# An attention block on one core: where the third load into a staging slot is issued, and how many fill products run

## The chip, the cores and the metric

The kernel runs on one core of a Trainium2 chip. The metric is the device time of one execution in microseconds (us). TensorE (PE) multiplies matrices and loads its weights beside them (PEld); VectorE (DVE), ScalarE (ACT) and GpSimd (POOL) work elementwise; SyncE (SP) issues nearly all transfers. Each engine executes its own list strictly in order and waits at semaphores for the others.

## The reference

The input x is 8 sequences of 512 rows of 256 numbers. Three steps follow each other:

```python
x = x + 0.5 * ffn(layernorm(x))      # layernorm again inside; weights quantised to -1, 0, 1
x = x + attention(layernorm(x))      # 16 query heads, 4 key/value heads, head size 128,
                                     # rotary positions, causal window of 64
x = x + 0.5 * ffn(layernorm(x))      # same ffn weights as in the first step
# ffn(x) = layernorm(x, gamma, beta) @ ternary(weight).T + bias
# attention: softmax(q k.T / sqrt(128), masked) v, then @ Wo + bo
```

## The kernel before, in words

The sequences ("batches") are worked off one after the other, and the work of neighbouring batches is interleaved. A batch is held transposed, features on the 128 partitions. Float32 operands of the large products are split into a rounded high part and a low remainder, and a product takes three matmuls (`three`, L567). The high part of a weight is made by ScalarE (`split_high`, L921), the low one by VectorE or GpSimd (L759, L1024).

The order of the work is written out by hand: one table of steps for each engine (TENSOR, VECTOR, SCALAR, GPSIMD, SYNC, L58 to L207), each with a prologue, a first batch, middle batches, a last batch and an epilogue. A step such as `Q2n` is "query head 2 of the next batch"; `c` is the current batch, `p` the previous, `i` and `f` occur once. `program` (L215) expands a table and the engine walks the list. Nothing is reordered at run time: a step that waits holds up all steps behind it on its engine.

The steps that matter here:

- `K0`, `Q0` to `Q15`: a projection on TensorE into one of two job banks in turn (`rope_job`, L645). VectorE multiplies it by the sine table (`rope_sin`, L802) and then the cosine table (`rope_cos`, L807). SyncE swaps the two halves of `rope_sin` with two DMAs of 128 KB into `rope_swap` (L548), and GpSimd adds both (`rope_add`, L1068). There are four sets of these buffers, used in turn: the fifth projection (Q3 in the prologue) may write its sine product once the first swap has landed, and its cosine product once the first add is done. A TensorE job waits until the job two places before it has been read out of its bank.
- `V00`, `V01`: values, read by ScalarE (L992) and VectorE (L812). `shift0` (L526) waits for V01's low part, then issues four DMAs of 192 KB that copy the values, moved by half a tile, into `v_odd`.
- `S` are scores, `exp` their exponentials on ScalarE, `inv` the reciprocal sums on VectorE, `probs` the normalisation on GpSimd, `T` the transposes of the probabilities on TensorE, `W` the product with the values, `O` the projection with Wo.
- Weights arrive in ten loads of 512 KB (`LOADS`, L414). Loads 0, 8 and 9 share one place, `stage_r` (the buffer `x_res`): load 0 holds the values' weights, load 8 a quarter of Wo, load 9 another. Load 8 may be issued when both splits of load 0 are done (`stage`, L494); the last of these is GpSimd's piece 1 (`w1i`). When load 8 has landed, ScalarE splits it in step `w11f`. The list of ScalarE goes on from the prologue into the first batch as `... w7i V01n | w11f exp0c mask2c exp1c V10c probsT0c`; that of VectorE as `... Q3n V01n | K1c Q4c max0c Q5c max1c inv0c Q6c inv1c w11f`; that of TensorE as `... Q2n Q3n V01n | K1c Q4c Q5c S0c S1c Q6c V10c T0c S2c Q7c W0c`.
- `fill0` to `fill5` (L727): products of ones or of the identity into `heads_p` which nobody reads. Their counts stand in FILLS; each is a float32 matmul that shows as two records. `last_fill` (L736) is a second such helper in the epilogue, between the two transposes `YT0p` and `YT1p`.

Of the kernel before, what the change touches and what calls it, by code (L numbers as in the profile page):

```python
# [37 lines left out]
P = 128  # L38
BATCHES, SEQ, E = 8, 512, 256
# [48 lines left out]
        T14c  # L88
    """,
    "epilogue": """  # L90
        O13p W14p T15p O14p W15p O15p YT0p last_fill0p YT1p FO0p FO1p
    """,
}
VECTOR = {
# [92 lines left out]
}  # L187
SYNC = {
    "prologue": """
        stage8i K0n Q0n Q1n Q2n Q3n shift0n  # L190
    """,
    "first": """
        K1c Q4c Q5c Q6c stage9f Q7c load0n K2c Q8c Q9c Q10c Q11c shift1c K3c
# [13 lines left out]
}  # L207


FILLS = (10, 3, 2, 2, 4, 4)  # L210
PARTS = {"p": -1, "c": 0, "n": 1}
WAVES = ("YT", "FO", "stats", "scale", "norm", "bias")

# [46 lines left out]
def block_kernel(nc, x, wq, wk, wv, wo, ffn_wT, columns, rows, rope_tables, mask, ident, out):  # L260
# [3 lines left out]
    with ExitStack() as ctx:  # L264
        def sb(name, shape, dt=F32):
            return ctx.enter_context(nc.sbuf_tensor(name, shape, dt))

        def psum(name, shape, dt=F32):
            return ctx.enter_context(nc.psum_tensor(name, shape, dt))
# [9 lines left out]
        w_tern = sb("w_tern", [P, EC, E], F32R)  # L279
# [33 lines left out]
        identf = sb("identf", [P, P])  # L313
# [15 lines left out]
        heads_p = psum("heads_p", [P, GROUP, 2, CHUNK])  # L329
# [158 lines left out]
        def flat_heads(ap):  # L488
            return ap.rearrange("p h c q -> p (h c q)")
# [16 lines left out]
        def _(sp):  # L506
# [13 lines left out]
            def store_half(x):  # L520

                _, m, b = x
                sp.wait_ge(ffn_added, FFN_OUT["FO2", m, b] + 1)
                sp.dma_start(out_t[b][:, 2 * m:2 * m + 2, :], x_res[:, 2 * m:2 * m + 2, :]).then_inc(out_stored, 16)

            def shift_values(x):  # L526

                _, half, b = x


                sp.wait_ge(v_lo, VALUES["V", (half, 1), b] + 1)
                cols = slice(half * NKV * HD // 2, (half + 1) * NKV * HD // 2)
                for s in range(2):
                    sp.dma_start(v_odd[0:CHUNK, s, :, cols].bitcast(F32),
                                 v_s[CHUNK:P, s, 0:BLOCKS - 1, cols].bitcast(F32)).then_inc(v_shifted, 16)
                    sp.dma_start(v_odd[CHUNK:P, s, :, cols].bitcast(F32),
                                 v_s[0:CHUNK, s, 1:BLOCKS, cols].bitcast(F32)).then_inc(v_shifted, 16)
# [28 lines left out]
        def _(pe):  # L566
# [160 lines left out]
            def fill(x):  # L727
# [3 lines left out]
                if x[1] >= 2:  # L731
                    pe.wait_ge(ident_in, 16)
                for _ in range(FILLS[x[1]]):
                    nc.tensor.matmul(flat_heads(heads_p[:, :])[:, 0:P], square, square, start=True, stop=True)

            def last_fill(_):  # L736

                dst = flat_heads(heads_p[:, :])
                for _ in range(6):
                    nc.tensor.transpose(dst[0:96, 0:P], identf[:, 0:96], identf[:, :])  # L740
                for _ in range(6):
                    nc.tensor.transpose(dst[0:64, 0:P], identf[:, 0:64], identf[:, :])
                for _ in range(3):
                    nc.tensor.matmul(dst[:, 0:96], identf[:, :], identf[:, 0:96], start=True, stop=True)
                for _ in range(5):
                    nc.tensor.matmul(dst[0:64, 0:E], w_tern[:, 0, 0:64], w_tern[:, 0, :], start=True, stop=True)
                for _ in range(5):
                    nc.tensor.matmul(dst[:, 0:P], w_tern[:, 0, 0:P], w_tern[:, 0, 0:P], start=True, stop=True)

            for x in PE_STEPS:  # L750
                {"S": scores, "T": transpose_probs, "W": values, "O": project, "K": rope_job, "Q": rope_job,
                 "V": value_job, "YT1": transpose_y, "YT2": transpose_y, "XT": transpose_y,
                 "FO1": ffn_job, "FO2": ffn_job, "total": sum_scale, "beta": beta_product,
                 "open": open_banks, "fill": fill, "last_fill": last_fill}[x[0]](x)


        @block.vector
        def _(dve):
            def split_low(x):  # L759
                n = x[1]  # L760
                _, where, dst = PIECES[n]
                dve.wait_ge(split_hi, HIGH[x] + 1)
                nc.vector.tensor_tensor(dst[1], where, dst[0].bitcast(F32), ALU.subtract).then_inc(split_lo_dve, 1)
# [395 lines left out]
```

## Time and profile before

| | us |
|---|---|
| median of 3 runs | 812.55 |
| lowest, highest | 811.66, 813.08 |
| profiled execution | 811.97 |
| its span, first to last instruction | 809.8 |
| TensorE busy | 790.4 (98%) |
| TensorE weight loads | 738.9 (91%) |
| VectorE, ScalarE, GpSimd busy | 634.3, 514.9, 452.8 |
| mean granted TensorE clock | 0.997 |

The profile is one execution; its times are counted from the first instruction. The page's chain of waits is followed back from the last instruction, and gives TensorE 90% of the span. TensorE is not evenly busy: the first and the last of the page's 40 slices, some 20 us each, are the least filled. Busy time of matmuls is modelled at its end, so that a group's duration holds a tail of some 0.2 us that overlaps the next group.

### The profile page before, as it was taken

How to read it: one execution, taken by the hardware profiler on the slowest of the kernel's cores; microseconds unless marked ns; L12 is line 12 of the kernel's file. 1: busy time of each engine (PE TensorE's matmuls, PEld its weight loads, DVE VectorE, ACT ScalarE, POOL GpSimd, SP SyncE). 2: the span in 40 equal slices, each digit the busy share in tenths (PEclk: the TensorE clock that was granted, in tenths of full speed). 3: DMA queues.
4: the chain of work that ended last, by engine and by line, in shares of the span. 5: the costliest groups of instructions: out<-in, count | busy, mean ns of one | idle time of the engine just before them, and what ended most of it. 6: DMA issues, size and time to landing. Idle time of an engine off the chain costs nothing.

```text
span 809.8 us, 16159 instructions
## 1 busy us (share of the span) xinstructions
PE 790.4 (98%) x5720; PEld 738.9 (91%) x5720; DVE 634.3 (78%) x1292; ACT 514.9 (64%) x1633; POOL 452.8 (56%) x437
## 2 busy tenths in 40 slices
PE   7799999999999999999999999999999999999986
PEld 6589999999999999999999999999999999999985
DVE  5588868978788887988778797797878887787754
ACT  4477765676666665676656766567665667575672
POOL 4578635576465645666446664557546464564542
PEclk9999999999999999999999999999999999999999
DMA  8463224341252423333233332344125242424300
GB/s 298 112 163 92 55 47 97 95 115 40 60 137 66 105 53 95 89 80 92 53 91 93 88 83 53 91 100 111 40 64 134 66 105 53 101 57 105 79 1 27
DMA packets 52431, 70.53 MB, mean 87 GB/s; under 512 B 7040, under 2 KB 30080, under 8 KB 52352
## 3 DMA queue, kind: packets, MB, share of 16 engines
q1 hardware_dynamic: 51792, 69.17, 35.2%
q8 instruction: 45, 0.74, 0.4%
q10 hardware_dynamic: 560, 0.34, 0.1%
q14 instruction: 34, 0.28, 0.1%
HBM read 10.76 MB, written 4.19 MB: 18 GB/s over the span
## 4 chain that ended last, share of the span: by engine, by line
PE 90%; POOL 3%; DVE 2%; ACT 2%; issue 2%; DMA 1%; SPq 0%; ACTq 0%; POOLq 0%; DVEq 0%
PE job_p L572 31%; PE attn_p L572 23%; PE scores_p L588 13%; PE heads_p L572 11%; PE probsT_p L626 7%; PE job_p L698 3%; PE job_p L687 3%; ACT headsT L960 1%; DVE headsT L780 1%; DMA k_s<-ffn_wT 1%; ACT y L982 1%; POOL q_s L1068 1%; POOL wq_s L1031 0%; POOL probs L1048 0%; ACT probs L938 0%
## 5 line engine op out<-in xcount | busy, mean ns | idle before, releaser
L1048 POOL TENSOR_TENSOR probs<-probs,inv_sum 128x512 f32<-128x512 f32 x128 | 134.4, 1050 | 198.3 <-DVE inv_sum L774 198.3
L938 ACT ACTIVATE probs<-scores_p,neg_max 128x128 f32<-128x128 f32 x512 | 181.0, 372 | 56.7 <-DVE neg_max L768 56.2
L572 PE MATMUL attn_p<-wo_s,headsT 128*128 128x256 f32 x1536 | 208.8, 285 | 5.0 <-DVE headsT L780 5.0
L572 PE MATMUL job_p<-xnT,wq_s 128*128 128x512 f32 x768 | 205.3, 403 | 0.6 <-DVE v_s L812 0.5
L572 PEld LDWEIGHTS attn_p<-wo_s,headsT 128*128 128x128 f32 x1536 | 195.7, 191 | 11.1 <-DVE headsT L780 6.6
L1068 POOL TENSOR_TENSOR q_s<-rope_cos,rope_swap 128x512 f32<-128x512 f32 x128 | 164.3, 1292 | 48.2 <-DMA rope_swap<-rope_sin 48.2
L960 ACT ACTIVATE headsT<-heads_p,columns_s 128x512 fp32r<-128x512 f32 x128 | 88.2, 689 | 154.5 <-PE heads_p L572 153.0
L572 PEld LDWEIGHTS job_p<-xnT,wq_s 128*128 128x128 f32 x768 | 136.6, 190 | 25.4 <-DVE v_s L812 0.9
L780 DVE SCALAR_TENSOR_TENSOR headsT<-heads_p,columns_s,headsT 128x512 fp32r<-128x512 f32 x128 | 95.7, 748 | 59.7 <-ACT headsT L960 58.2
L588 PE MATMUL scores_p<-k_s,q_s 128*128 128x128 f32 x1024 | 135.0, 275 | 0.0
L802 DVE SCALAR_TENSOR_TENSOR rope_sin<-job_p,columns_s,rope_t 128x512 f32<-128x512 f32 x160 | 119.0, 744 | 14.0 <-PE job_p L572 10.1
L588 PEld LDWEIGHTS scores_p<-k_s,q_s 128*128 128x128 f32 x1024 | 125.9, 192 | 1.6
L807 DVE SCALAR_TENSOR_TENSOR rope_cos<-job_p,columns_s,rope_t 128x512 f32<-128x512 f32 x160 | 118.7, 742 | 0.5 <-POOL k_s L1068 0.5
L938 ACT ACTIVATION_READ_ACCUMULATOR probs<-scores_p,neg_max 128x1 f32 x512 | 108.1, 211 | 0.0
L768 DVE TENSOR_REDUCE neg_max<-scores_p 128x4 f32<-128x512 f32 x128 | 86.8, 682 | 15.8 <-PE scores_p L588 15.8
L786 DVE TENSOR_TENSOR probsT<-probsT_p,probsT 128x512 fp32r<-128x512 f32 x128 | 86.6, 677 | 4.4 <-ACT probsT L966 4.4
L966 ACT ACTIVATE probsT<-probsT_p 128x512 fp32r<-128x512 f32 x128 | 76.4, 597 | 20.8 <-PE probsT_p L626 20.7
L572 PE MATMUL heads_p<-probsT,v_s 128*128 128x256 f32 x480 | 79.0, 284 | 0.0
L953 ACT ACTIVATE scores_p<-mask_s 128x512 f32<-128x512 bf16 x128 | 77.5, 607 | 0.7
L626 PE MATMUL probsT_p<-identf,probs 128*128 128x128 f32 x512 | 77.0, 273 | 0.4 <-POOL probs L1048 0.2
L1068 POOL TENSOR_TENSOR k_s<-rope_cos,rope_swap 128x512 f32<-128x512 f32 x32 | 41.3, 1292 | 49.3 <-DMA rope_swap<-rope_sin 49.3
L572 PEld LDWEIGHTS heads_p<-probsT,v_s 128*128 128x128 f32 x480 | 66.7, 191 | 0.5 <-DVE probsT L786 0.4
(87 smaller groups left out, 930.7 us busy)
## 6 DMA issues: line engine op xcount, KB each, us to landing
rope_swap<-rope_sin SPq DMA_DIRECT2D x320, 128.0 KB, 2.3
v_odd<-v_s SPq DMA_DIRECT2D x64, 192.0 KB, 3.2
out<-x_res SPq DMA_DIRECT2D x16, 256.0 KB, 2.5
x_in<-x SPq DMA_DIRECT2D x15, 256.0 KB, 3.2
staging<-wo SPq DMA_DIRECT2D x2, 512.0 KB, 10.7
staging<-wq SPq DMA_DIRECT2D x2, 512.0 KB, 10.8
x_res<-wo SPq DMA_DIRECT2D x2, 512.0 KB, 4.1
x_res<-wv SPq DMA_DIRECT2D x1, 512.0 KB, 7.3
```

Of the source, the lines that this page charges most:

```text
L572: mm = nc.tensor.matmul(dst, a(p), b(q), start=first and clears and i == 0, stop=last and i == 2, skip_group_check=True)
L588: mm = nc.tensor.matmul(dst[:, 2 * cc + pair, :], q_s[g % 2][:, c, 2 * pair:2 * pair + 2, :], k_s[:, g % 2, w0:w0 + P], start=False, stop= ...
L626: mm = nc.tensor.transpose(probsT_p[:, k, :], probs[:, x[1] % 2, k, :], identf[:, :])
L768: nc.vector.tensor_reduce(neg_max[:, i, :], scores_p[i][:, :, :], AX.X, ALU.max, negate=True).then_inc(max_ready, 1)
L780: nc.vector.scalar_tensor_tensor(out=flat_heads(headsT[:, 1]), in0=flat_heads(heads_p[:, :]), scalar=bv_s[:, g:g + 1], in1=flat_heads(head ...
L786: nc.vector.tensor_tensor(probsT[:, 1, :, :], probsT_p[:, :, :].rearrange("p (c a) n -> p c (a n)", c=2), probsT[:, 0, :, :].bitcast(F32), ...
L802: nc.vector.scalar_tensor_tensor(out=rope_sin[:, r, :], in0=bank[:, :], scalar=bias, in1=sin_t, op0=ALU.add, op1=ALU.mult).then_inc(rope_s ...
L807: nc.vector.scalar_tensor_tensor(out=rope_cos[:, r, :], in0=bank[:, :], scalar=bias, in1=cos_t, op0=ALU.add, op1=ALU.mult).then_inc(rope_c ...
L938: ins = nc.scalar.activation(probs[:, i, k, :], scores_p[i][:, k, :], ACT.Exp, bias=neg_max[:, i, k:k + 1], accum_out=row_sum[:, i, k:k + 1])
L960: nc.scalar.activation(flat_heads(headsT[:, 0]), flat_heads(heads_p[:, :]), ACT.Identity, bias=bv_s[:, g:g + 1]).then_inc(heads_hi, 1)
L1048: nc.gpsimd.tensor_tensor(probs[:, i, :, :], probs[:, i, :, :], inv_sum[:, i, :].unsqueeze(2).to_broadcast([P, 4, P]), ALU.mult).then_inc( ...
L1068: nc.gpsimd.tensor_tensor(roped(x), as_roped(x, rope_cos[:, r, :]), as_roped(x, rope_swap[:, r, :]), ALU.add).then_inc(rope_added, 1)
```

## The change

It has three parts. In SyncE's prologue, the issue of load 8 (`stage8i`) moves from ahead of the five swaps K0n, Q0n to Q3n and of `shift0n` to behind them. In FILLS, fill1 goes from 3 products to 1 and fill2 from 2 to 1. In the epilogue `last_fill` with its 25 products and transposes of several shapes gives way to a plain `fill6` of 12 products of the identity.

```diff
@@ TENSOR, epilogue
-        O13p W14p T15p O14p W15p O15p YT0p last_fill0p YT1p FO0p FO1p
+        O13p W14p T15p O14p W15p O15p YT0p fill6p YT1p FO0p FO1p
@@ SYNC, prologue
-        stage8i K0n Q0n Q1n Q2n Q3n shift0n
+        K0n Q0n Q1n Q2n Q3n shift0n stage8i
@@
-FILLS = (10, 3, 2, 2, 4, 4)
+FILLS = (10, 1, 1, 2, 4, 4, 12)
@@ TensorE's helpers
-            def last_fill(_):
-
-                dst = flat_heads(heads_p[:, :])
-                for _ in range(6):
-                    nc.tensor.transpose(dst[0:96, 0:P], identf[:, 0:96], identf[:, :])
-                for _ in range(6):
-                    nc.tensor.transpose(dst[0:64, 0:P], identf[:, 0:64], identf[:, :])
-                for _ in range(3):
-                    nc.tensor.matmul(dst[:, 0:96], identf[:, :], identf[:, 0:96], start=True, stop=True)
-                for _ in range(5):
-                    nc.tensor.matmul(dst[0:64, 0:E], w_tern[:, 0, 0:64], w_tern[:, 0, :], start=True, stop=True)
-                for _ in range(5):
-                    nc.tensor.matmul(dst[:, 0:P], w_tern[:, 0, 0:P], w_tern[:, 0, 0:P], start=True, stop=True)
-
```

## Rows read from the trace of the kernel before

**Rows 1.** The page: chain of waits, by engine.
```profile
PE 90%; POOL 3%; DVE 2%; ACT 2%; issue 2%; DMA 1%; SPq 0%; ACTq 0%; POOLq 0%; DVEq 0%
```
**Rows 2.** Timeline of SyncE's queue: start, us, line, transfer, count.
```profile
29.26 0.37 SPq L500 DMA_DIRECT2D x_res<-wo  x1
29.67 7.60 SPq L548 DMA_DIRECT2D rope_swap<-rope_sin  x10
37.51 0.65 SPq L534 DMA_DIRECT2D v_odd<-v_s  x1
```
**Rows 3.** Timelines of GpSimd and VectorE (in brackets: idle before, releaser).
```profile
27.86 1.31 POOL L1031 TENSOR_TENSOR wv_s<-x_res,wv_s 128x512 fp32r<-128x512 f32 x1
34.83 1.27 POOL L1068 TENSOR_TENSOR k_s<-rope_cos,rope_swap 128x512 f32<-128x512 f32 x1 [5.66 <-DMA rope_swap<-rope_sin]
40.98 2.42 POOL L1031 TENSOR_TENSOR wq_s<-staging,wq_s 128x1024 fp32r<-128x1024 f32 x1
...
25.69 0.74 DVE L802 SCALAR_TENSOR_TENSOR rope_sin<-job_p,columns_s,rope_t 128x512 f32<-128x512 f32 x1
31.34 0.74 DVE L807 SCALAR_TENSOR_TENSOR rope_cos<-job_p,columns_s,rope_t 128x512 f32<-128x512 f32 x1
34.85 0.75 DVE L802 SCALAR_TENSOR_TENSOR rope_sin<-job_p,columns_s,rope_t 128x512 f32<-128x512 f32 x1 [2.77 <-DMA rope_swap<-rope_sin]
```
**Rows 4.** Timeline of TensorE, same columns.
```profile
32.14 1.69 PE L572 MATMUL job_p<-wv_s,xnT 128*128 128x256 f32 x12
36.94 2.66 PE L572 MATMUL job_p<-xnT,wk_s 128*128 128x512 f32 x6 [3.11 <-DVE rope_cos L807]
42.74 1.95 PE L588 MATMUL scores_p<-k_s,q_s 128*128 128x128 f32 x16
47.70 0.66 PE L626 MATMUL probsT_p<-identf,probs 128*128 128x128 f32 x4
49.00 1.64 PE L572 MATMUL job_p<-xnT,wq_s 128*128 128x512 f32 x6
```
**Rows 5.** Stretches: us, busy of PE, PEld, DVE, ACT, POOL; clock, DMA share, GB/s.
```profile
38.00:40.00 2.00, 2.00 (x6) 1.51 (x6) 0.36 (x1) 0.00 (x0) 2.00 (x3) 0.50 0.83 186
60.00:100.00 40.00, 40.00 (x303) 37.89 (x302) 34.69 (x77) 28.26 (x91) 31.53 (x29) 1.00 0.33 74
```
**Rows 6.** Transfers: issue to landing in us, of 29 to 29.6, 37.4 to 40.2, 49.9 to 50.5.
```profile
x_res<-wo SPq DMA_DIRECT2D x1, 512.0 KB, 4.4
v_odd<-v_s SPq DMA_DIRECT2D x4, 192.0 KB, 3.2
x_res<-wo SPq DMA_DIRECT2D x1, 512.0 KB, 3.8
```
**Rows 7.** The swap buffers in 20 to 60 us.
```profile
DMA to landing us min/median/max: 2.2/2.6/4.5
```
**Rows 8.** Timeline of ScalarE.
```profile
33.87 0.60 ACT L992 ACTIVATE v_s<-job_p 128x512 fp32r<-128x512 f32 x1 [5.36 <-PE job_p L572]
34.36 1.05 ACT L925 ACTIVATE wo_s<-x_res 128x1024 fp32r<-128x1024 f32 x1
44.56 0.37 ACT L938 ACTIVATE probs<-scores_p,neg_max 128x128 f32<-128x128 f32 x1 [9.14 <-DVE neg_max L768]
```
**Rows 9.** Timeline of TensorE and ScalarE at the start.
```profile
6.94 1.63 PE L734 MATMUL heads_p<-y 128*128 128x128 f32 x6
8.36 1.06 PE L687 MATMUL job_p<-identf,y 128*128 128x128 f32 x4
11.33 0.66 PE L687 MATMUL job_p<-identf,y 128*128 128x128 f32 x4 [1.14 <-ACT y L982]
6.75 1.09 ACT L982 ACTIVATE y<-x_in,shift,rstd 128x256 f32<-128x256 f32 x2 [0.37 <-POOL shift L1042]
```
**Rows 10.** Timeline of TensorE at the end.
```profile
796.75 1.70 PE L572 MATMUL attn_p<-wo_s,headsT 128*128 128x256 f32 x12 [1.56 <-DVE headsT L780]
802.83 0.63 PE L687 MATMUL job_p<-identf,y 128*128 128x128 f32 x4 [0.90 <-ACT y L982]
```

More of the change, by code:

```diff
@@ L753, in _ @@
                  "FO1": ffn_job, "FO2": ffn_job, "total": sum_scale, "beta": beta_product,
-                 "open": open_banks, "fill": fill, "last_fill": last_fill}[x[0]](x)
+                 "open": open_banks, "fill": fill}[x[0]](x)
         @block.vector
```

## The prediction

> **What bounds the kernel now.** I read the page's chain of waits first, then stretches of the trace, then each engine's timeline from 20 to 60 us. The chain gives TensorE 90% [rows 1], and from 47.7 us on it is busy without a gap (40.00 of 40.00 us in the stretch to 100) [rows 5]. So a microsecond is only won or lost where TensorE stands still: in the first 48 us, and in the epilogue. What sets the whole time is when the first transpose of probabilities, T0c, starts: 47.70 us [rows 4]; everything behind it keeps its order and its distance.
>
> Before T0c there is one long stall. Load 8 goes out at 29.26, after GpSimd's last split of load 0 (27.86 + 1.31), and the first swap only at 29.67, behind it [rows 2, 3]. That swap had been possible since K0n's sine product, 25.69 + 0.74 = 26.43. It lands so late that GpSimd waits 5.66 us, to 34.83, and VectorE 2.77 us, to 34.85, for the fifth projection's sine product [rows 3]; so TensorE idles 3.11 us ahead of K1c, from 33.83 to 36.94 [rows 4]. After this gap the granted clock falls to 0.50, the 1.2 GHz level (the stretch from 38 to 40), and K1c takes 2.66 us instead of the 1.64 that six such matmuls take at 1.00 [rows 4, 5].
>
> **The change part by part.** *The swaps.* They go out as soon as their sine products exist. A pair costs SP two issues of some 0.6 us (one takes 0.65 in the shift) [rows 2], and a swap lands 2.2 to 2.6 us after its issue, the least and the median [rows 7]. K0n's lands at 26.5 + 0.6 + 2.3 = 29.4 instead of 34.8. GpSimd is busy with its split until 29.2, so the adds begin at 29.4, 5.4 us earlier. VectorE ends Q2n's cosine product at 31.34 + 0.74 = 32.08 [rows 3] and can do Q3n's two at once (0.67 us apart), to 33.53. TensorE ends V01n at 33.83 and goes on with K1c at 33.7: 3.2 us won. The clock has no reason to fall there. K1c and Q4c take 1.4 us each at the full clock (Q4c waits until 35.2 for V01n's low part); Q5c needs K1c's cosine product (36.7) and ends at 38.2. Q3n's swap lands at 35.8 and its add ends at 37.1, in time. S0c starts at 38.2 instead of 42.74, 4.5 us earlier [rows 4]. S1c, Q6c and V10c follow to 43.0: 0.9, half of a group of two less its tail, 1.4, and 1.5 as V01n without its tail [rows 4].
>
> *What load 8 is now late for.* It is issued behind the shift. V01n's high part ends at 33.87 + 0.60 [rows 8], its low part, priced as VectorE's like products at 0.75 [rows 3], at 35.2. The shift's four issues take 4 x 0.65 = 2.6 us [rows 2], so load 8 goes out at 37.8 instead of 29.26. Alone it took 4.4 us to land, its successor 3.8 [rows 6]; here 768 KB of values are ahead of it, the last of them landing at 37.2 + 3.2 = 40.4. Low bound for its landing 37.8 + 3.8 = 41.6; high bound, all of it behind the shift's end and half a swap's lateness more, 43.4. I take 37.8 + 4.5 = 42.3, nearest to the row of the same load.
>
> Nobody needs this piece of Wo soon, but ScalarE's list has its split, w11f, ahead of exp0c. Today w11f runs at 34.36, covered by the wait for the scores, and ScalarE then idles 9.14 us [rows 8]. Now ScalarE stands at w11f from 34.5 to 42.3, although the row maxima of S0c are ready by 40.0. exp0c starts 0.95 us after w11f, at 43.25. Behind exp0c wait inv0c, probs0c and T0c: from 44.56 to 47.70 they took 3.14 us [rows 4, 8]. VectorE and GpSimd offer no shorter way; GpSimd's splits w8i and w7f, 2.4 us each [rows 3], end at 41.9. T0c: 43.25 + 3.14 = 46.4, 1.3 us earlier than now. Of the 4.5 us won at S0c, 3.2 go back at the new wait. With the bounds of the landing: 45.7 to 47.5, a gain of 2.0 to 0.2.
>
> *TensorE meanwhile.* It has nothing from 43.0 to 46.4: the stall of 3.11 us has become one of about 3.4 us, further on. A gap of 3.11 was followed by the low clock; gaps of 1.56 and 0.90 us at the end, with packed work behind the first at its usual 1.70 us, were not [rows 4, 5, 10]. A gap longer than the one that cost the clock most likely costs it again. K1c lost 1.0 us of 2.66 to it and the work behind K1c lost more; half the speed over some 3.4 us, which the low level lasted, is 1.7 us, of which some 0.2 fall on waits that are there anyway: +1.5. Bounds: 0, if the clock stays, and 2.9, if the low level ends later because it begins inside the gap. In the profiled execution the fall cost less, since GpSimd's splits, which end at 45.7 now, would have held T0c until 46.85 anyway.
>
> By the Trainium skill (TensorE: Matmul & The Clock Gate, Part 1), the chip's looks at TensorE's activity are free-running, not tied to the kernel's start; the trace, one execution, neither shows nor denies it. By that rule the fall comes in some executions and not in others, for both kernels, and the sum would lie between the forecast and the first rival.
>
> *The first fills.* Records of fill1 take 0.23 to 0.27 us there. Six hold TensorE from 6.94 to 8.36, while y for YT0n is ready at 6.75 + 1.09 = 7.84 [rows 9]. Two end at 7.5, so YT0n starts at 8.0 and ScalarE and all after it get 0.2 to 0.4 us; none if records are already fast by then. fill2's two missing records lie in the gap ahead of YT1n (1.14 us) and cost nothing themselves. Taken: -0.2.
>
> *The last fill.* Now 29 records, from 798.7 to 801.9; fill6 has 24 of 0.11 us and ends at 801.4. The next transposes wait for y until 802.83 [rows 10]. The old fill was hidden and so is the new: 0. The gap grows from 0.9 to 1.4, below the 1.56 that cost no clock; if it does, FO1p is 1.1 us longer.
>
> Sum on the profiled 811.97 (span 809.8 and 2.17 around it): -1.3 + 1.5 - 0.2 = 0. The profiled execution lies 0.6 under the median, and as the difference is what I predict, I put it on the median: 812.6.
>
> **The rivals.** *1. The clock stays up after the new gap.* For it: at 1.56 us it stayed [rows 10], and the limit may be a matter of luck for a single gap. Against: 3.4 is longer than 3.11. Then -1.3 - 0.2 = -1.5: 811.1, and with the early landing 810.4.
>
> *2. The start stays at the low clock (slower).* The granted column reads 1.00 from the first microsecond, but four transposes take 1.06 us at 8.36 and 0.66 at 11.33 [rows 9]: the level is 1.2 GHz up to then, and rises ahead of 11.33. Before the rise TensorE works without a gap from 6.94 to past 9.4; fill0's ten products, ahead of that, brought none, since fill1's records still take twice their later time [rows 9]. The change takes six records out of this block and opens gaps at 7.5 to 8.0 and from 9.5 to 11.0. If the rise then comes only after the packed stretch from 11 to 17, YT1n takes 0.4 more and the product for beta 0.9 more, both on the path to x_mid, and open0i and fill4i then delay XT0n by some 0.2: +1.5, bound 3. It decides if the first ten products alone don't bring the rise. With the forecast's other terms: 814.3; with a clock that stays up at T0c, 812.8. By the Trainium skill (same page, Part 4: PE-mode transpose) a transpose does not count as busy TensorE like a matmul. By that rule the thinned block, half of it transposes, would hold still less, which speaks for this rival; no row isolates it.
>
> *3. Load 8 lands late.* The swaps of K1c and Q4c and the shift share the engines with it; at 43.4 T0c is at 47.5: +1.1, 813.7. By the Trainium skill (DMA: Bandwidth & Descriptors, Queues, rings and completion order) each engine consumes a queue's descriptors in ring order; the trace agrees, as K0n's swap behind load 8 took 4.5 instead of 2.3 us [rows 7].
>
> *4. The wait at w11f doesn't hold exp0c*, because the landing is much earlier than I think. exp0c would start at 40.1 and T0c at 43.3: -4.4, without a gap, 808.0. Against: the issue cannot come before V01n's low part, 35.2, and four issues.
>
> **How the numbers follow.** Forecast 0.40, rival 1 0.25, rival 2 0.19, rival 3 0.08, rival 4 0.08. A measurement can tell about 0.2%, 1.6 us. Faster by more than that is rival 4 and well over half of rival 1, with the early landings: 0.24. Slower is most of rival 2 and a part of rival 3: 0.22. Within: 0.54. Range 810.4 (rival 1 with the early landing) to 814.9 (rival 2 with a later landing); the likeliest case alone 811.8 to 813.5.
>
> **What would show it.** In the profile after: K0n's add at about 29.4 and no idle ahead of K1c (33.7); S0c at 38.2; load 8 issued at 37.8; ScalarE idle some 7 us ahead of the split of `x_res` and exp0c right behind it; TensorE idle 3 us or more ahead of T0c at 46.4; a clock of 0.50 right after. The second transposes at the start (now 11.33) taking 1.06 instead of 0.66 us would show rival 2. I am wrong if TensorE's gap ahead of T0c is under 1 us, or if S0c doesn't come 4 us earlier.

## The result: 0.31% slower, and the profile after

The changed kernel takes 814.93 us (median of 8 runs, 813.63 to 815.93), the kernel before in the same session 812.30 (8 runs, 811.66 to 813.28). The ratio is 1.0031, 95% interval 1.0020 to 1.0042: 2.6 us slower, beyond the 0.2% that a measurement can tell. The time lies at the upper edge of the stated range (814.9), and not in the "no change" that the forecast held likeliest. The profiled execution, 815.93 us, is the slowest of the eight; it has a span of 813.8 us against 809.8, so it shows more of the loss (4.0 us) than the median does.

SyncE's queue in the changed kernel (start, us, line, transfer, count), and how long load 8 took from issue to landing:

```profile
27.48 7.64 SPq L548 DMA_DIRECT2D rope_swap<-rope_sin  x10
36.25 0.65 SPq L534 DMA_DIRECT2D v_odd<-v_s  x1
38.97 0.58 SPq L500 DMA_DIRECT2D x_res<-wo  x1
39.66 10.49 SPq L548 DMA_DIRECT2D rope_swap<-rope_sin  x8
...
x_res<-wo SPq DMA_DIRECT2D x1, 512.0 KB, 6.7
```

Against [rows 2] the swaps begin 2.2 us earlier, load 8 (the last `x_res` row) goes out 9.7 us later, and it takes 6.7 us instead of 4.4 [rows 6]. TensorE of the changed kernel:

```profile
8.04 1.11 PE L687 MATMUL job_p<-identf,y 128*128 128x128 f32 x4
11.05 1.12 PE L687 MATMUL job_p<-identf,y 128*128 128x128 f32 x4 [1.48 <-ACT y L968]
20.25 0.63 PE L687 MATMUL job_p<-identf,y 128*128 128x128 f32 x4 [1.19 <-ACT y L968]
33.18 1.69 PE L572 MATMUL job_p<-wv_s,xnT 128*128 128x256 f32 x12
34.70 1.55 PE L572 MATMUL job_p<-xnT,wk_s 128*128 128x512 f32 x6
39.24 1.95 PE L588 MATMUL scores_p<-k_s,q_s 128*128 128x128 f32 x16
49.54 1.11 PE L626 MATMUL probsT_p<-identf,probs 128*128 128x128 f32 x4 [5.45 <-POOL probs L1034]
52.01 2.91 PE L572 MATMUL job_p<-xnT,wq_s 128*128 128x512 f32 x6
54.71 0.96 PE L572 MATMUL heads_p<-probsT,v_s 128*128 128x256 f32 x6
```

K1c now follows V01n without a gap (34.70, no bracket) at full speed, and the scores start at 39.24 instead of 42.74. But T0c has 5.45 us of idle time ahead of it and starts at 49.54 instead of 47.70 [rows 4]. Who is waited for stands in ScalarE's timeline:

```profile
34.90 0.60 ACT L978 ACTIVATE v_s<-job_p 128x512 fp32r<-128x512 f32 x1 [5.38 <-PE job_p L572]
45.70 1.06 ACT L911 ACTIVATE wo_s<-x_res 128x1024 fp32r<-128x1024 f32 x1 [10.20 <-DMA x_res<-wo]
46.66 0.35 ACT L924 ACTIVATE probs<-scores_p,neg_max 128x128 f32<-128x128 f32 x1
```

ScalarE waits 10.20 us for load 8; exp0c comes right behind its split, at 46.66, although VectorE's maxima were there at about 41. The clock, in stretches (us, busy of PE, PEld, DVE, ACT, POOL, granted clock, DMA share, GB/s):

```profile
47.60:49.60 2.00, 0.06 (x1) 0.07 (x2) 1.42 (x3) 1.97 (x10) 1.16 (x2) 0.62 0.00 0
49.60:54.40 4.80, 4.80 (x18) 4.32 (x19) 3.51 (x6) 3.46 (x14) 4.80 (x4) 0.50 0.51 129
60.00:100.00 40.00, 40.00 (x298) 37.72 (x298) 34.73 (x77) 27.35 (x84) 29.03 (x27) 1.00 0.36 80
```

The clock falls inside the gap and stays at 0.50 (1.2 GHz) for some five microseconds of packed work (in finer stretches, from about 48.1 to 54.9 us): Q7c takes 2.91 us instead of 1.64 [rows 4], and W0c starts at 54.71. The kernel before has these two rows for XT0n, the transposes that stand at 20.25 above, and for W0c:

```profile
19.24 0.63 PE L687 MATMUL job_p<-identf,y 128*128 128x128 f32 x4 [1.20 <-ACT y L982]
50.61 0.98 PE L572 MATMUL heads_p<-probsT,v_s 128*128 128x256 f32 x6
```

The 4.1 us between the two starts of W0c are the whole difference of the spans. From 60 us on TensorE is as full as in [rows 5].

So the profiled loss of 4.0 us has three parts: 1.0 us at the start (XT0n at 20.25 instead of 19.24), 0.8 more until T0c (1.84 in all), 2.3 from T0c to W0c under the low clock (5.17 us instead of 2.91).

### The profile page after: what moved, and what is told of

Its sections match the earlier page's. It is cut to its first block, busy times and chain, and to the rows that moved or that the text cites. A ratio compares the mean times of both kernels' runs of the same rounds, so it can differ in the third digit from the quotient of the medians.

```text
span 813.8 us, 16140 instructions
## 1 busy us (share of the span) xinstructions
PE 791.1 (97%) x5710; PEld 739.0 (91%) x5710; DVE 634.2 (78%) x1292; ACT 515.0 (63%) x1633; POOL 452.2 (56%) x437
## 4 chain that ended last, share of the span: by engine, by line
PE 90%; POOL 3%; DVE 2%; ACT 2%; issue 2%; DMA 0%; ACTq 0%; POOLq 0%; DVEq 0%
PE job_p L572 30%; PE attn_p L572 23%; PE scores_p L588 13%; PE heads_p L572 11%; PE probsT_p L626 7%; PE job_p L698 3%; PE job_p L687 3%; ACT headsT L946 1%; DVE headsT L766 1%; ACT y L968 1%; POOL q_s L1054 1%; POOL wq_s L1017 0%; DVE parts L846 0%; DMA x_in<-x 0%; POOL probs L1034 0%
## 5 line engine op out<-in xcount | busy, mean ns | idle before, releaser
L1054 POOL TENSOR_TENSOR q_s<-rope_cos,rope_swap 128x512 f32<-128x512 f32 x128 | 164.2, 1291 | 49.9 <-DMA rope_swap<-rope_sin 49.9
L626 PEld LDWEIGHTS probsT_p<-identf,probs 128*128 128x128 f32 x512 | 59.9, 141 | 8.8 <-POOL probs L1034 6.3
```

Source lines behind the costliest of these rows:

```text
L626: mm = nc.tensor.transpose(probsT_p[:, k, :], probs[:, x[1] % 2, k, :], identf[:, :])
L1054: nc.gpsimd.tensor_tensor(roped(x), as_roped(x, rope_cos[:, r, :]), as_roped(x, rope_swap[:, r, :]), ALU.add).then_inc(rope_added, 1)
```

## The experiments

My theory when I made them: the stall has moved to the split of load 8 on ScalarE; that wait, made longer by the shared transfers, and the low clock behind it make most of the loss; the fewer first fills add the rest through the clock at the start. The rivals: the fills make it all; transfers hold T0c in any case; T0c's lateness counts and not the clock. All medians below stand beside runs of the kernel before on the same chip: 812.49 for `move_only`, `fills_only`, `late_split` and `load_between`, 812.15 for `move_filled`, `move_hold`, `fill2_long` and `last_fill_only`, 812.11 for `after_between` and `between_fill2`. Where two kernels of different groups are compared, the figure is the difference of what each gained or lost against its own neighbours. The intervals are 95%.

**The parts of the change, alone.** `move_only`:

```diff
-        stage8i K0n Q0n Q1n Q2n Q3n shift0n
+        K0n Q0n Q1n Q2n Q3n shift0n stage8i
```

> Only the issue of load 8 moves behind the swaps and the shift; all fills as before. Theory A (my reading of the profile after: T0c is held by the split of load 8 on ScalarE, the stall only moves, and the low clock after it lasts longer): TensorE idles 3.5 to 5.5 us ahead of T0c, T0c starts at 47.5 to 48.5, and the time is 0.8 to 2.5 us above the kernel before; fill terms absent, records at full clock from about 10 us. Rival B (the fills cost the time, the move gains about a microsecond): -0.5 to -2 us.

Measured: 814.82, ratio 1.0031 (1.0019 to 1.0042), +2.3 us. TensorE idles 5.43 us ahead of T0c, which starts at 48.63; ScalarE, T0c, W0c and the clock in this kernel:

```profile
44.80 1.06 ACT L925 ACTIVATE wo_s<-x_res 128x1024 fp32r<-128x1024 f32 x1 [10.18 <-DMA x_res<-wo]
...
48.63 1.12 PE L626 MATMUL probsT_p<-identf,probs 128*128 128x128 f32 x4 [5.43 <-POOL probs L1048]
52.79 0.87 PE L572 MATMUL heads_p<-probsT,v_s 128*128 128x256 f32 x6
...
48.60:51.00 2.40, 2.37 (x11) 2.37 (x12) 1.83 (x4) 2.28 (x8) 2.40 (x2) 0.50 0.54 113
```

T0c is 0.9 us later than in the kernel before, and W0c comes 4.16 us behind it instead of 2.91, 1.25 us more under the low clock: 2.2 us together, near the median's 2.3. The move by itself makes the larger part of the loss; rival B, that it gains, falls.

`fills_only`:

```diff
-FILLS = (10, 3, 2, 2, 4, 4)
+FILLS = (10, 1, 1, 2, 4, 4)
```

> Only fill1 and fill2 shrink (3 to 1 and 2 to 1 products). Theory A: the second transposes at about 11 us take 1.1 instead of 0.66 us in most executions, everything behind comes 0.5 to 1.2 us later: +0.3 to +1.2 us. Rival B: this part alone makes the whole loss, +2 us or more. Rival C: fewer fills gain 0.2 to 0.4 us.

Measured: 813.46, ratio 1.0013 (1.0005 to 1.0022), +1.0 us: theory A. Its start shows how. In this execution the clock did rise early (fill0's 20 records take 4.25 us; in the changed kernel they take 4.63, all at the low level), and then it fell again, in the thinned block:

```profile
1.04 4.25 PE L734 MATMUL heads_p<-y 128*128 128x128 f32 x20 [1.04 <-DVE y L884]
...
4.50:7.00 2.50, 1.17 (x9) 1.01 (x9) 2.25 (x12) 0.88 (x3) 0.89 (x2) 1.00 0.91 187
7.00:10.00 3.00, 1.72 (x8) 1.24 (x7) 1.66 (x7) 1.91 (x5) 2.27 (x3) 0.69 1.03 386
10.00:13.00 3.00, 2.11 (x7) 1.92 (x8) 0.77 (x2) 1.79 (x5) 0.00 (x0) 0.50 1.03 394
...
10.89 1.12 PE L687 MATMUL job_p<-identf,y 128*128 128x128 f32 x4 [1.48 <-ACT y L982]
```

So rival 2 of the prediction came true, at two thirds of its price of +1.5, and one way to it was not foreseen: an early rise, and a fall when the thinned block follows. TensorE is busy 1.17 of 2.50 and then 1.72 of 3.00 us there. In the changed kernel's own profile it went the foreseen way: fill0 brings no rise, and the two groups of transposes take 1.11 and 1.12 us.

`fill2_long` asks whether fill1's missing products or the empty gap ahead of YT1n cost the clock:

```diff
-FILLS = (10, 3, 2, 2, 4, 4)
+FILLS = (10, 1, 4, 2, 4, 4)
```

> Kernel before with fill1 at 1 product, as in the change, but fill2 at 4 instead of 1. Theory A (the loss of the fewer fills is the low clock from 11 us on, as the gap ahead of YT1n is too empty): the transposes at 11 us take 0.66 us again, and the time is -0.4 to +0.2 us against the kernel before. Rival B (fill1's two missing products already cost the clock): +0.7 to +1.3 us, as with both fills short.

Measured: 812.16 against 812.15, ratio 0.9998 (0.9989 to 1.0008). The transposes take 0.66 us again, and start 0.33 us before those of [rows 9]:

```profile
8.89 1.91 PE L734 MATMUL heads_p<-identf 128*128 128x128 f32 x8
11.00 0.66 PE L687 MATMUL job_p<-identf,y 128*128 128x128 f32 x4 [0.20 <-ACT y L982]
```

Theory A: with the gap filled the clock is up at 11 us, and the loss is gone. The third of a microsecond that fill1 gives shows in this one execution but not clearly in the median.

`last_fill_only`:

```diff
-        O13p W14p T15p O14p W15p O15p YT0p last_fill0p YT1p FO0p FO1p
+        O13p W14p T15p O14p W15p O15p YT0p fill6p YT1p FO0p FO1p
-FILLS = (10, 3, 2, 2, 4, 4)
+FILLS = (10, 3, 2, 2, 4, 4, 12)
```

> Only the last fill is exchanged for fill6. Theory A: it is hidden before and after, the second transposes of the epilogue take 0.63 us at the full clock, within 0.4 us of the kernel before. Rival B: the gap behind the shorter fill costs the clock in a part of the executions, +0.5 to +1.2 us.

Measured: 811.74, ratio 1.0000 (0.9990 to 1.0009). The exchange is free. The epilogue has 1.27 us ahead of the second transposes, at full clock:

```profile
798.01 2.84 PE L734 MATMUL heads_p<-identf 128*128 128x128 f32 x24
802.13 0.63 PE L687 MATMUL job_p<-identf,y 128*128 128x128 f32 x4 [1.27 <-ACT y L982]
```

The start of this execution answers a question about the first fills. It has the old counts, and the clock rose early as in `fills_only`, but it did not fall again; both groups of transposes run at full clock, and XT0n starts at 18.25 instead of 19.24. It is one execution against one:

```profile
1.04 4.44 PE L734 MATMUL heads_p<-y 128*128 128x128 f32 x20 [1.04 <-DVE y L884]
7.79 0.65 PE L687 MATMUL job_p<-identf,y 128*128 128x128 f32 x4
10.35 0.66 PE L687 MATMUL job_p<-identf,y 128*128 128x128 f32 x4 [1.46 <-ACT y L982]
```

**Is it ScalarE's wait?** `late_split` has the move, and ScalarE's split of load 8 further back:

```diff
-        w11f exp0c mask2c exp1c V10c probsT0c mask3c
+        exp0c mask2c exp1c w11f V10c probsT0c mask3c
```

> The move as in the change, fills as before, and on ScalarE the split of load 8 (w11f) goes behind exp0c, mask2c and exp1c. Theory A (the wait of ScalarE at that split is what takes back the gain): exp0c starts at 40 to 41, T0c at 43.3 to 44, no idle time over 1 us ahead of T0c, no low clock there, and the time is 3 to 4.5 us under the kernel before. Rival B (transfers, that is the values' shift or the swaps' landing, hold T0c or W0c anyway): less than 1.5 us under the kernel before.

Measured: 809.17, ratio 0.9966 (0.9954 to 0.9979): 3.3 us under the kernel before, 5.7 under the move alone. Nothing on SyncE differs from `move_only`, and load 8 still takes 6.1 us to land. The wait at the split is the cause. TensorE and ScalarE:

```profile
43.38 0.66 PE L626 MATMUL probsT_p<-identf,probs 128*128 128x128 f32 x4 [0.26 <-POOL probs L1048]
47.96 0.98 PE L572 MATMUL heads_p<-probsT,v_s 128*128 128x256 f32 x6 [1.64 <-DVE probsT L786]
...
40.08 0.37 ACT L938 ACTIVATE probs<-scores_p,neg_max 128x128 f32<-128x128 f32 x1 [5.56 <-DVE neg_max L768]
44.16 1.06 ACT L925 ACTIVATE wo_s<-x_res 128x1024 fp32r<-128x1024 f32 x1 [0.51 <-DMA x_res<-wo]
```

T0c is 4.3 us earlier than before, as the fourth rival had worked it out for a wait that doesn't hold. Of this, 1.64 us are lost ahead of W0c: VectorE's own split of load 8 stands ahead of the low part of the transposed probabilities on its list, and now has to wait 1.40 us for ScalarE's, which comes late with the load.

**Does the load have to be behind the shift?** `load_between`, the splits as before:

```diff
-        stage8i K0n Q0n Q1n Q2n Q3n shift0n
+        K0n Q0n Q1n Q2n Q3n stage8i shift0n
```

> Load 8 is issued behind the five swaps but ahead of the shift, fills as before. Theory A: it goes out at about 34.1 and lands at 38 to 39.5, before the maxima of S0c are there; S0c at about 38.5, T0c at 43.3 to 44, 3 to 4.5 us under the kernel before. Rival B (landing takes 6 us or more wherever it is issued near the swaps, since they share the engines): landing after 40, T0c at 45 or later, under 2 us won.

Measured: 807.75, ratio 0.9948 (0.9935 to 0.9962), 4.7 us under the kernel before. Load 8 goes out at 34.07, when the swaps are issued and V01n's low part is not yet there; it lands after 4.2 us; ScalarE has split it by the time the maxima are ready. TensorE has no stall ahead of T0c, and the clock stays up until the last microseconds of the kernel:

```profile
34.07 0.53 SPq L500 DMA_DIRECT2D x_res<-wo  x1
...
x_res<-wo SPq DMA_DIRECT2D x1, 512.0 KB, 4.2
...
38.32 1.06 ACT L925 ACTIVATE wo_s<-x_res 128x1024 fp32r<-128x1024 f32 x1 [3.84 <-DMA x_res<-wo]
40.05 0.37 ACT L938 ACTIVATE probs<-scores_p,neg_max 128x128 f32<-128x128 f32 x1 [0.67 <-DVE neg_max L768]
...
43.19 0.66 PE L626 MATMUL probsT_p<-identf,probs 128*128 128x128 f32 x4
...
37.00:43.00 6.00, 6.00 (x40) 5.18 (x39) 5.04 (x9) 3.98 (x15) 5.67 (x4) 1.00 1.03 261
```

**How much is the clock?** `move_filled` is the move alone, with 20 products nobody reads in the gap:

```diff
-        K1c Q4c Q5c S0c S1c Q6c V10c T0c S2c Q7c W0c T1c S3c K2c
+        K1c Q4c Q5c S0c S1c Q6c V10c fill6c T0c S2c Q7c W0c T1c S3c K2c
-FILLS = (10, 3, 2, 2, 4, 4)
+FILLS = (10, 3, 2, 2, 4, 4, 20)
```

> The move alone, fills as before, and 20 products of the identity (40 records of 0.11 us, some 4.5 us) on TensorE between V10c and T0c, in the gap of 5.4 us. Theory A (half of the move's loss is the low clock after the gap): T0c starts where it did with the move alone (48.6), but at the full clock, and the time falls by 1.7 to 3 us against the move alone, to about 812 to 813, no change against the kernel before. Rival B (the late T0c itself is the loss): no more than 0.5 us under the move alone.

Measured: 811.93, ratio 0.9999 (0.9989 to 1.0008). Against the neighbours that is -0.2 us, where the move alone has +2.3: about 2.6 us won back, as theory A had it.

```profile
43.15 4.63 PE L734 MATMUL heads_p<-identf 128*128 128x128 f32 x40
48.06 0.66 PE L626 MATMUL probsT_p<-identf,probs 128*128 128x128 f32 x4 [0.28 <-POOL probs L1048]
50.97 0.98 PE L572 MATMUL heads_p<-probsT,v_s 128*128 128x256 f32 x6
...
48.00:54.00 6.00, 5.94 (x40) 5.22 (x41) 5.43 (x10) 4.62 (x18) 6.00 (x6) 1.00 0.53 134
```

The two profiled executions differ by 2.6 us in span. T0c starts 0.6 us earlier here, for load 8 landed after 6.0 us and not 6.7; 1.25 us go with the clock between T0c and W0c (2.91 us instead of 4.16). The remaining 0.8 us lie behind W0c, where both have the full clock, and stay unexplained: the distance from W0c to the end is 759.6 us in one and 758.8 in the other, with 759.2 in the kernel before. That the clock is what the products buy shows in the other executions too: their mean granted clock is 0.998 to 1.000 in all twelve, against 0.991 to 0.998 in the eleven of the move alone, of which the profiled one is the highest. Work that does nothing buys back all that the move lost. It is no cure: the T0c at 48.06 is still later than the 47.70 of before.

**Why does load 8 land so late?** `move_hold`, in `swap_halves`:

```diff
+                if x == ("K", 1, 0):
+                    sp.wait_ge(staged[8], 16)
```

> The move alone, and SyncE waits until load 8 has landed before it issues the swap of K1c and what is behind it; so nothing is queued behind load 8. Theory A (transfers issued behind load 8 share the engines with it and stretch its landing): it lands 4.5 to 5.3 us after its issue instead of 6.7, T0c comes 1.4 to 2.2 us earlier than with the move alone, and the time falls by 1 to 2.5 us against it. Rival B (only what is ahead, the shift, stretches it): still 6.3 to 6.9 us, and the time is the same as the move alone or above.

Measured: 811.64, ratio 0.9994 (0.9984 to 1.0003). Against the neighbours that is -0.5 us, 2.8 under the move alone's +2.3, a little more than theory A allowed.

```profile
x_res<-wo SPq DMA_DIRECT2D x1, 512.0 KB, 4.7
...
46.45 0.66 PE L628 MATMUL probsT_p<-identf,probs 128*128 128x128 f32 x4 [3.47 <-POOL probs L1050]
46.40:52.00 5.60, 5.55 (x39) 4.89 (x40) 5.03 (x9) 4.22 (x17) 5.60 (x4) 1.00 0.69 182
```

With nothing behind it the load lands after 4.7 us, although the shift is ahead of it as in the move alone. With K0n's swap 0.4 us behind it and nothing ahead it took 4.4 [rows 6], with the swaps ahead and the shift from 1.2 us behind, 4.2. Only with the shift's four copies ahead and the swaps from 0.7 us behind were there 6.0 to 6.7, in all four kernels with that order. T0c starts at 46.45, where the prediction had put it, and the gap of 3.47 us did not cost the clock in this execution. That was probably the exception: the mean granted clock of the other ten executions is 0.991 to 0.998, nine of them under the 0.998 that is the lowest with the gap filled. No trace of them shows where it fell. What the median won is therefore mostly the earlier T0c, 2.2 us.

**The change with one step moved.** `after_between` is the changed kernel, fills and all, with load 8 ahead of the shift:

```diff
-        K0n Q0n Q1n Q2n Q3n shift0n stage8i
+        K0n Q0n Q1n Q2n Q3n stage8i shift0n
```

> The changed kernel with one step moved: load 8 goes ahead of the shift instead of behind it, everything else of the change stays (fewer first fills, fill6). Theory A (the wait at w11f and the low clock behind it made the move's loss, the fills the rest): 3 to 4.3 us under the kernel before, that is 0.5 to 1.5 us above the same order with the old fills (-4.7). Rival B (the fewer fills cost nothing once the stall is gone): -4.5 us or better.

Measured: 808.27, ratio 0.9953 (0.9940 to 0.9965), -3.8 us. That one step turns +2.6 into -3.8. It stays some 0.9 us behind `load_between` against its own neighbours, which is what the fewer fills cost alone; its second transposes take 1.12 us again, and the clock there is 0.50:

```profile
10.00:13.00 3.00, 1.97 (x7) 1.79 (x8) 0.88 (x2) 1.79 (x6) 0.00 (x0) 0.50 1.05 397
```

`between_fill2` is the best version: `load_between` with the fills of `fill2_long`.

> Kernel before with load 8 between the swaps and the shift, fill1 at 1 product and fill2 at 4. Theory A: both gains add up, YT0n starts 0.35 us earlier with the clock up at 11 us: -4.7 to -5.3 us against the kernel before. Rival B (fill1's 0.35 us is lost again in part of the executions): -4 to -4.7 us.

Measured: 807.06, ratio 0.9936 (0.9924 to 0.9949), 5.1 us under the kernel before, and 7.7 under the changed one, each taken against its own neighbours. The expectation's two ranges met near this value, so the run does not show that fill1's third of a microsecond adds up; it shows that nothing is lost.

## Why the prediction was right in its mechanism and wrong in its size

- *The swaps*: right. K1c follows V01n without a gap at full clock, and S0c came 3.5 us earlier against the clock of the trace, 4.5 us once the 1.0 us lost at the start is taken out, as worked out. K0n's add itself came at 32.31, later than the 29.4 worked out (30.4 with the start's loss), as the second of its two transfers landed after 4.2 us and not 2.3. There was slack for it.
- *What load 8 is now late for*: the mechanism was right, the wait of ScalarE at w11f, ahead of exp0c; `late_split` shows it. This is also the step that failed, in its size. I took 4.5 us for the landing with 43.4 as the upper end; it was 6.7 us, so 44.8 in the move alone and 45.7 in the changed kernel. I had priced what was ahead of the load and, but for half a swap's lateness, not what is issued behind it; `move_hold` shows that without it the landing is 4.7 us and T0c is at 46.45. The row that the 4.5 leaned on was not "alone" either: K0n's swaps went out 0.4 us behind it. Beyond that point each term followed, with 4.1 us from the landing to T0c forecast: T0c comes 3.8 us after the landing in both (48.63 and 49.54).
- *TensorE meanwhile*: right, the fall of the clock came. Between T0c and W0c it cost 1.25 us in the profile of the move alone and 2.3 in that of the changed kernel, where the low level lasted from inside the gap to past 54 us, longer than the 3.4 us of before; +1.5 had been forecast, 2.9 was the bound. The rule "longer than 3.11" was weaker than it looked. The traces have a fall behind gaps of 2.83 (`fills_only`), 3.11, 3.13 (`fill2_long`), 3.33 (`last_fill_only`), 5.43 and 5.45 us, and none behind one of 3.47 (`move_hold`), whose other executions mostly show a lower mean clock. So around 3 us it depends on the execution, and in these traces a fall is the common case. That agrees with the sentence of the Trainium skill (TensorE: Matmul & The Clock Gate, Part 1) that the chip's looks are free-running, though no run here isolates it; had I weighed it more, the forecast would have been nearer to the first rival and no better.
- *The first fills*: wrong in sign. Taken as -0.2, they cost +1.0 (`fills_only`). This was rival 2, with a chance of 0.19 and a price of +1.5; it should have been the likelier case, since the block it thins out was the one ahead of the rise of the clock, and the gain to set against it was 0.2 to 0.4 us. Rival 2's point of decision, whether the ten products bring the rise alone, was incomplete: in the changed kernel's profile they did not, in `fills_only` they did, and the thinned block lost it again, which the old fills did not do in `last_fill_only`.
- *The last fill*: right, 0 (`last_fill_only`).
- *The sum*: forecast 0. In the medians the move gave +2.3 where the terms -1.3 and +1.5 stood, and the fills +1.0 where -0.2 stood. In the trace of the move alone the first of these terms is +0.9, for the late landing, and the second +1.25. Alone they add up to 3.3, the whole change has 2.6; the intervals of the three are wide enough for this, and whether one loss covers a part of the other was not tried.
- Rival 3, load 8 late, had the right mechanism with an end of 43.4 that was still too early. Rivals 1 and 4 didn't come true. "Within 0.2%" was held likeliest and missed; slower by more had 0.22. The upper end of the range, 814.9, stood for rival 2 with a later landing, and that is what came, but that it was enough is partly luck: both rivals at their full prices give 812.6 + 1.7 + 1.1 = 815.4, rival 2 cost less than its price, and the landing was later than its bound.

## What to carry to other kernels

When a transfer is moved back in a queue, look for the first instruction that stands behind its consumer on the consumer's engine, not for the first that needs the data: here nobody needed the load for many microseconds, and a split at the head of ScalarE's list held the softmax for it. Price its landing with what is issued on both sides of it. And a fill that looks hidden may be what keeps TensorE's clock up; it is only free to go when the gap that it leaves is filled otherwise.

## What the runs showed of the hardware that I had not expected

- A load of 512 KB took 4.2 to 4.7 us from issue to landing in eight kernels, among them one with four copies of 192 KB ahead of it and nothing behind, and 6.0 to 6.7 in the four that had these copies ahead and swaps of 128 KB from 0.7 us behind. The Trainium skill (DMA: Bandwidth & Descriptors, Queues, rings and completion order) says that each engine consumes its descriptors in ring order, but also that a later one may finish its write before an earlier one, so that a delay by later transfers does not go against it. The traces show the whole time, not the cause inside the engines.
- The clock's level at the start differs between executions of nearly the same start: it is up before fill0's end in `fills_only`, where it then falls for some 7 us, and in `last_fill_only`, where it stays; it rises ahead of 11.33 us in the kernel before [rows 9], and only at about 14 us in the changed kernel. There the granted column shows 1.00 all the same; the durations of the records tell.
